# GNN and expert layer on one core: block bounds loaded inside ScalarE's blocks, the padding issued by SyncE, VectorE's weight splits spread over eight turns

## The reference

```python
x = x + gnn(layernorm(x), adj, W, a)          # attention over the 64 nodes, elu
x = x + ffn(layernorm(x), Wg, bg, W1, b1, W2, b2)
# ffn: 8 experts, the two best per token by x @ Wg.T + bg, softmax of the two scores
#   h = relu(x @ W1[e].T + b1[e])             # 128 -> 512
#   y = h @ W2[e].T + b2[e]                   # 512 -> 128
#   out += weight[token, e] * y
```

## Time and profile before

| | |
|---|---|
| three runs | 449.86, 452.69 and 452.71 us, median 452.69 |
| profiled execution | 451.05 us, its span 449.2 us |
| mean granted TensorE clock | 0.967 |
| busy: PE, PEld, DVE, ACT, POOL | 91%, 69%, 80%, 71%, 65% of the span |
| start of the last `yb` | 421.08 us |

### The profile page before, as it was taken

How to read it: one execution, slowest core, us unless ns; L and a number is a source line. 1 busy time by engine, 2 the same in 40 slices (tenths; PEclk the granted TensorE clock), 3 DMA queues, 4 the chain that set the end, 5 groups by cost and what they waited for, 6 DMA issues and landing times.

```text
span 449.2 us, 9041 instructions
## 1 busy us (share of the span) xinstructions
PE 409.9 (91%) x2231; PEld 311.3 (69%) x2246; DVE 360.4 (80%) x1410; ACT 320.1 (71%) x760; POOL 291.1 (65%) x292
## 2 busy tenths in 40 slices
PE   7889889889999888899999999999999999999960
PEld 3666666666666666688888877777887878878620
DVE  5579999999998898789888697697877768777933
ACT  2578887888888897488898677677767767877400
POOL 1041677777777777677778777676666657566761
PEclk9889999999999998799999999999999999999995
DMA  6995334433333344443532333333233232277699
GB/s 168 271 387 202 96 107 122 118 101 102 100 103 99 99 125 119 123 110 118 173 95 72 106 112 98 97 95 93 84 88 106 67 112 88 68 273 236 233 322 325
DMA packets 56291, 63.03 MB, mean 140 GB/s; under 512 B 7744, under 2 KB 40896, under 8 KB 56000
## 3 DMA queue, kind: packets, MB, share of 16 engines
q1 hardware_dynamic: 35728, 33.28, 24.9%
q0 software_dynamic: 9344, 20.10, 13.4%
q10 hardware_dynamic: 11184, 9.26, 6.9%
HBM read 27.28 MB, written 26.94 MB: 121 GB/s over the span
## 4 chain that ended last, share of the span: by engine, by line
PE 58%; DVE 21%; issue 6%; ACT 6%; DMA 3%; SPq 2%; POOL 2%; ACTq 1%; DVEq 0%; POOLq 0%
PE bank L1440 7%; PE bank L1424 7%; PE bank L1437 7%; PE bank L1438 7%; PE bank L1428 6%; PE bank L1425 6%; PE bank L1408 3%; PE bank L1416 3%; PE bank L1386 3%; PE bank L1384 3%; DVE xn L1062 2%; DVE bn L897 2%; DVE score L1039 2%; DVE neg_max L1044 2%; PE bank L1325 2%
## 5 line engine op out<-in xcount | busy, mean ns | idle before, releaser
L510 POOL DMA_INDIRECT expert_slots<-rows,slot_i x128 | 127.3, 994 | 56.6 <-issue 35.0
L1437 PE MATMUL bank<-hh,w_hi 128*128 128x512 f32 x144 | 61.0, 424 | 0.0
L702 ACT ACTIVATE yb<-bank,b_sb 128x512 f32<-128x512 f32 x36 | 24.8, 689 | 49.6 <-PE bank L1440 49.6
L1424 PE MATMUL bank<-xh,w_hi 128*128 128x512 f32 x144 | 58.8, 408 | 0.8 <-ACT xh L687 0.8
L1440 PE MATMUL bank<-hl,w_hi 128*128 128x512 f32 x144 | 57.7, 401 | 0.1
L1438 PE MATMUL bank<-hh,w_lo 128*128 128x512 f32 x144 | 57.8, 401 | 0.0
L1428 PE MATMUL bank<-xl,w_hi 128*128 128x512 f32 x144 | 57.2, 397 | 0.0
L1425 PE MATMUL bank<-xh,w_lo 128*128 128x512 f32 x144 | 57.1, 397 | 0.0
L526 POOL DMA_INDIRECT moe_rows<-hexp,ysi x40 | 43.8, 1095 | 18.3 <-issue 9.5
L526 POOL DMA_INDIRECT moe_rows<-hrelu,ysi x40 | 41.1, 1027 | 19.4 <-issue 11.8
L1138 DVE CAST hh<-z 128x512 fp32r<-128x512 f32 x36 | 17.1, 475 | 44.9 <-ACT z L692 44.6
(11 more groups left out here) (166 smaller groups left out, 1052.0 us busy)
## 6 DMA issues: line engine op xcount, KB each, us to landing
rows<-xn SPq DMA_DIRECT2D x32, 256.0 KB
xs<-expert_slots SPq DMA_DIRECT2D x27, 260.0 KB
x_all<-x SPq DMA_DIRECT2D x16, 256.0 KB, 3.8
w_raw<-w_t SPq DMA_DIRECT2D x2, 2048.0 KB, 12.9
w_raw<-moe_rows SPq DMA_DIRECT2D x16, 256.0 KB, 4.1
out<-x_all ACTq DMA_DIRECT2D x16, 256.0 KB, 5.0
xs<-expert_slots ACTq DMA_DIRECT2D x11, 260.0 KB
w_hi<-moe_rows SPq DMA_DIRECT2D x9, 256.0 KB, 3.8
```

The lines of the kernel that those rows point to most:

```text
L510: nc.gpsimd.indirect_dma_start(out=slots, out_offset=bass.IndirectOffsetOnAxis(ap=slot_i[q][:, k * SUB + j:k * SUB + j + 1], axis=0), in_= ...
L702: nc.scalar.activation(yb[:, :], ps_y[:, :], ACT.Identity, bias=b2_sb[:, e:e + 1]).then_inc(yb_ok, 1)
L1424: nc.tensor.matmul(ps_h[c][:, :], w1_hi[:, e, chunk], xh[:, :], start=True, stop=False)
L1437: nc.tensor.matmul(ps_y[:, :], w2_hi[:, e, c, :], hh[:, c, :], start=c == 0, stop=False)
```

## The change

Three edits. `pad` gets the engine as an argument, and SyncE issues pads 2 to 7, each just before its loop over an expert's blocks. Its wait is now for one pad more than before, all that have been issued. ScalarE loads the bound of the next expert inside the loop, in every block of experts 0 to 6, between `round_x` and `result`; only the bound of expert 0 is still loaded outside. VectorE's `low_halves` becomes two calls of `low_half(e, layer)`, and of the four experts' eight instructions one stands behind each of turns 4 to 11.

```diff
+        def pad(eng, e):
+            n = eng.value_load(count_i[0:1, e:e + 1], min_val=0, max_val=TOKENS)
+            eng.dma_start(slots[bass.ds(n + e * CAP, GROUP), :].rearrange("(p s) r -> p s r", s=SUB),
+                          pad_rows[:, e % 2, :, :]).then_inc(pads_out, 16)
...
             for e in range(E - 1):
                 bounds.append(block_bound(sp, e))
-                sp.wait_ge(pads_out, 16 * max(e + 1, 2))
+                sp.wait_ge(pads_out, 16 * min(e + 2, E))
+                if e + 2 < E:
+                    pad(sp, e + 2)
                 with sp.Fori(bounds[e], bounds[e + 1]) as i:
...
                 if 3 <= i < 5:
-                    pad(i - 3)
+                    pad(act, i - 3)
                 result(i, i // 2)
-            bounds = [SURE_BLOCKS]
+            bounds = [SURE_BLOCKS, block_bound(act, 0)]
             for e in range(E):
-                bounds.append(block_bound(act, e))
-                if 0 < e < E - 1:
-                    pad(e + 1)
                 with act.Fori(bounds[e], bounds[e + 1]) as i:
...
                         load_block(act, row, i + LEAD)
+                    else:
+                        until = block_bound(act, e + 1)
                     result(i, e)
+                bounds.append(until)
...
-            with dve.Fori(1, BUFS + 1) as m:
+            with dve.Fori(1, 3) as m:
                 for b in range(BUFS):
                     turn(BUFS * m + b, b, m)
-                low_halves(m + 3)
-            with dve.Fori(BUFS + 1, QUADS) as m:
+                    low_half(m * 2 + (2 + b // 2), b % 2)
+            with dve.Fori(3, QUADS) as m:
                 for b in range(BUFS):
                     turn(BUFS * m + b, b, m)
```

More of the change, by code:

```diff
@@ L740, in drain @@
                 result(1, 0)
[L742 to L746, removed]
             by_steps(act, step, GROUPS)
@@ L1098, in step, with low_half @@
                     low_halves(t - LOW)
-            def low_halves(e):
[L1102 to L1109, removed]
+            def low_half(e, layer):
+                dve.wait_ge(hi_ok, e + 1)
+                raw, hi, lo = ((w1_raw, w1_hi, w1_lo), (w2_raw, w2_hi, w2_lo))[layer]
+                raw, hi, lo = (v[:, bass.ds(e, 1), :].rearrange("p e h -> p (e h)") if layer == 0 else
+                               v[:, bass.ds(e, 1), :, :].rearrange("p e c d -> p (e c d)") for v in (raw, hi, lo))
+                last = nc.vector.tensor_tensor(lo, raw, hi.bitcast(F32), ALU.subtract)
+                if layer == 1:
+                    last.then_inc(lo_ok, 1)
+            def low_halves(e):
+                for layer in range(2):
+                    low_half(e, layer)
             def low_x(i):
```

## The result

| | before | the change |
|---|---|---|
| first session, five runs each | 449.86 to 452.94 us, median 452.69 | 443.3 to 447.94 us, median 446.4 |
| ratio, 95% interval | | 0.9883 [0.9851, 0.9915] |
| second session | 446.84 to 452.8 us, median 450.67 (17 runs) | 445.18 to 449.73 us, median 447.22 (12 runs) |
| ratio, 95% interval | | 0.9926 [0.9896, 0.9957] |
| profiled execution, its span | 451.05, 449.2 us | 447.94, 446.1 us |

The change is faster, by 3.1 us in the profiled executions.

A forecast was written before the change was run, and what follows sets the result against it. TensorE was taken to bound the blocks, ScalarE's boundary work delaying it. 451.05 - 2.96, all else at nothing, gave 448.1 us; from the median 449.7. The forecast was the middle, 448.9 us, range 446.5 to 451.5.

The forecast's parts named there:

- The bound and the six boundaries: TensorE bounds the blocks at 6.46 us each; six expert boundaries with a pad fall from 0.62 to 0.13, saving 2.96 us.
- the remaining 0.13: Cost in us left at each pad boundary, as at expert 7, read as TensorE's own load of the bound.
- the 0.30 at expert 0: Boundary to expert 0 stays at 0.30 us because ScalarE's load there still stands outside the loop.
- Together they are the 1.23 us: ScalarE's two register loads, pad issue and register work between `yb` and `z` make up the 1.23 us idle before `z`.
- edit 1: The ScalarE edit, taking bound load and pad issue off six boundaries: 2.96 us saved, bounds 1.9 to 3.87.
- The third rival: ScalarE's loop end, branch and first wait keep a third to half of the cost; saves 1.5 to 2.0 us; 12%.
- The load in each block at nothing: ScalarE's added bound load per block, about 0.5 us, costs nothing within its idle; at most 12 us if uncovered.
- The wait-queue rule of the Trainium skill: The sequencer queues a waiting activation and goes on; loads and pads would then already be hidden, saving 0 instead of 2.96.
- SyncE and VectorE at nothing: SyncE's pads and bound loads cost 0; VectorE's low parts spread singly cost 0, bounds -0.2 and +0.2 us.
- The second rival: Pads in SyncE's queue hold back block loads; slower, 3.6 us back or up to 468 us in all; 4%.
- The end: The 28.2 us from the last `yb` on, DMA share 0.97, move forward with the blocks, give or take 0.7 us.
- which runs to forecast from: Sum is 448.1 us from the profiled execution, 449.7 from the median of 452.69; the middle, 448.9, was forecast.

The follow-up runs named there:

- e1: The change without its VectorE edit (low parts in pairs as before): ratio 0.9943 [0.9911, 0.9975] to the unchanged kernel, median 447.38 us, blocks 168.97 us.
- e3: The unchanged kernel with ScalarE's bound loaded inside the blocks, pads left on ScalarE: ratio 0.9958 [0.9921, 0.9994], blocks 169.39 us.
- e4: The change with ScalarE's bounds still loaded at the boundaries and VectorE as before, pads on SyncE: ratio 0.9957 [0.9927, 0.9988], blocks 169.21 us.
- e6: The change with TensorE's bound also loaded inside blocks and the table_ok wait moved ahead: ratio 0.9900 [0.9860, 0.9939], median 446.52 us, blocks 167.96 us.
- e7: The unchanged kernel with one more unused bound load on ScalarE at each of six pad boundaries: 454.42 us, blocks 175.21 us, single execution.
- e8: The change with four bound loads instead of one in each block of experts 0 to 6 on ScalarE: blocks 168.91 us, single execution.
- e9: The change with eight bound loads instead of one in each block of experts 0 to 6 on ScalarE: blocks 178.15 us, single execution.
- e2: The unchanged kernel with only VectorE's low parts changed: ratio 1.0037 [1.0011, 1.0064], blocks 172.27 us.
- e10: The change with five more 260 KB transfers behind each of six pads in SyncE's queue: blocks 169.00 us, single execution.

## Why the prediction was right, and where it was off

**The bound and the six boundaries: right.** Forecast 2.96 us from the blocks, measured 3.05. Against its own profiled execution the sum gave 448.1, measured 447.94. e1, e3 and e4 show that the cost was the work on ScalarE between `yb` and `z`, and e6 shows that the remaining 0.13 was TensorE's own load. For the 0.30 at expert 0 the prediction had the wrong reason (see e6).

**"Together they are the 1.23 us": right as a sum, misleading as a cause.** I priced edit 1 as a whole and gave its lower bound as a third staying at each boundary. The parts don't add up: without the bound's load 2.74 us go, without the pads 2.92, and with neither 3.05. The loss starts only where `z` is 0.6 to 0.7 us late (e3, e7). The third rival, some of ScalarE's branch work staying and costing, falls with e3: four times the idle that stayed costs 0.05 us a boundary.

**The load in each block at nothing: right, with more cover than I gave it.** e8 hides 2.1 us of loads with 1 us to spare. e9's 4.2 us and more are seen.

**The wait-queue rule of the Trainium skill** ("Perfetto Trace Analysis", Per-engine timelines) came out half right here. The sequencer does run ahead of the engine: the load at 388.3 precedes `xh` of its block, at 389.34. But it did not run ahead of the wait in front of `yb`, or the pads would have cost nothing before, and e7's extra load nothing either.

**SyncE and VectorE at nothing: right.** The change's own rows show it for the pads in SyncE's queue, e2 for the low parts. The second rival, the pads holding back block loads, needed 5.5 us for a pad and a load together. Its mechanism is seen in e10, with six times the bytes. In the change the pad goes out 1.9 us behind one load, lands 2.1 to 2.7 us later, and the next load is issued 4.6 us or more behind it.

**The end: within its 0.7 us.** It took 28.60 instead of 28.12 us, and the stretch ahead of block 7 was 0.54 us shorter. Neither can be put down to the change. The stretch behind the last `yb` took 28.1 to 29.8 us over the twelve profiled executions, 28.9 in e2, where ScalarE is as before. `yb` of block 7 started between 234.55 and 236.72.

**The step that was off: which runs to forecast from.** The sum was to stand halfway between the profiled execution and the median of three runs, and 446.4 is 0.1 us below my range and 2.5 below the forecast. I had given 81% to a change within 1%; the first session says 1.2%, the second 0.7%. A profiled execution and a median don't compare well here: in all seven sets of five or more runs of the change and its variants, the profiled execution was slower than the set's median, by 0.5 to 2.5 us, while that of before was 1.64 faster. Like with like, the sum holds: 448.1 against 447.94 for the profiled ones, and 450.67 - 2.96 = 447.7 against 447.22 for the medians of the second session.

The first session's ratio of 0.9883 is 5.3 us, of which the boundaries explain 3.05. The time goes with the mean granted clock. Over 33 runs of the unchanged kernel in one session it went from 446.16 us at a mean granted clock of 0.983 to 452.82 at 0.966. With one slope for all timed runs (123 runs of nine kernels, each kernel with a level of its own), 0.001 of mean clock goes with 0.28 us, and the runs scatter by 0.9 us around it. With the clock so taken out, the change is 3.7 +- 0.9 us faster by the first session and 3.3 +- 0.6 by the second, e1 3.0 +- 0.6, e2 0.0 +- 0.6. Those five first runs of the change had a mean clock of 0.974, before's average is 0.972, so their own clock goes with only some 0.6 us of the 5.3. The rest is that the first session's five runs of before came out at 451.9 us on average, where 50 others average 450.2. Why stays open, for their clock was not listed. Nor is it shown that the clock is the cause. Where it falls is seen by stretch, here in the profiled executions of before and then of the change (columns as in the earlier trace rows):

```profile
0.00:181.70 181.70, 159.11 (x1042) 115.54 (x1057) 157.48 (x962) 140.65 (x460) 111.63 (x124) 0.97 0.47 146
181.70:202.20 20.50, 19.42 (x96) 15.39 (x97) 17.21 (x74) 12.94 (x25) 14.09 (x14) 0.83 0.39 106
202.20:421.00 218.80, 218.63 (x1063) 174.78 (x1061) 171.49 (x355) 165.81 (x276) 152.29 (x144) 1.00 0.38 118
```

```profile
0.00:181.70 181.70, 157.20 (x1068) 112.88 (x1068) 158.98 (x969) 141.06 (x462) 112.31 (x125) 0.99 0.48 147
181.70:202.70 21.00, 20.48 (x89) 16.48 (x90) 16.78 (x68) 13.18 (x24) 14.21 (x15) 0.76 0.36 107
202.70:417.50 214.80, 214.71 (x1058) 175.38 (x1057) 170.34 (x353) 165.34 (x275) 148.57 (x142) 1.00 0.39 118
```

Up to the last `yb` all of the lower clock lies before 203 us, in two places: the attention stage, and where that stage drains into the blocks, where TensorE spends a part of the time at 1.2 GHz. As an estimate from these rows, length times what is missing to 1.00, before lacks about 5 us of full clock in the first and 3.5 in the second, the change about 2 and 5. The tail behind the last `yb` has a granted clock of 0.78 over 28.2 us, about 6 us. In the blocks the clock is 2.4 GHz throughout, in both, so the blocks' distances are free of it.

## What to carry to other kernels

Where one engine is the bound and its neighbours idle 1.5 us a block, look for the places where the period breaks: sum the periods against the steady one, and price each place by what stands there. In this kernel a neighbour's work cost next to nothing up to 0.6 us and beyond that nearly in full, so two edits that each bring it under the threshold are worth as much as both. A register load that stood between the loops was free inside the loop, ahead of the last wait, on the bounding engine too: e6 gained there all that the boundaries still cost. The room is limited, as e9 shows. And a median of many landings can hide the few that matter, as in e10.

## What the runs showed that was not expected

- ScalarE's sequencer reaches a register load 3.2 us before the next `yb`, ahead of activations that are still to run, but stays behind the semaphore wait of `yb`.
- In e6 TensorE's register load stands in the program in front of the fourth matmul of `result`. At the block before the boundary to expert 1 that matmul starts at 253.81 and the load at 252.26, while the transposes run. With its register work it takes 0.6 us, and the blocks stay at 6.46 us: the sequencer has that much lead there.
- A whole kernel's time can vary by 6.7 us from run to run (446.16 to 452.82) with identical work, and goes with its mean granted clock. In the two profiles read for it, the clock fell only ahead of the blocks and in the tail.
